# Row statistics over two rows at once, and the inverse root on VectorE instead of GpSimd, in the last layer of a graph network

## The reference, cut to what matters

```python
for l in range(4):                                  # 50000 nodes, 128 features, 25000 edges + self loops
    m = x @ weight[l]
    agg = segment_sum(m[src], dst, num_segments=50000)
    gi, gh = agg @ w_ih.T + b_ih, x @ w_hh.T + b_hh  # 3 x 128 each: r, z, n
    r, z = sigmoid(i_r + h_r), sigmoid(i_z + h_z)
    n = tanh(i_n + r * h_n)
    x = (1 - z) * n + z * x
y = x0 + (x + x0)                                   # x0: the input
out = (y - mean(y)) / sqrt(var(y) + 1e-5)           # over the 128 features
```

## Time and profile before

| | |
|---|---|
| median of three runs | 2330.25 us (2329.54 to 2333.68) |
| span of the profiled execution | 2327.4 us |
| what the median has beyond that span | 2.85 us |
| TensorE, VectorE busy | 96%, 93% of the span |
| ScalarE, GpSimd busy | 79%, 74% of the span |
| in 1900 to 2200 us, last layer: TensorE, VectorE | 294.04, 298.21 of 300 us |
| in the same stretch: ScalarE, GpSimd | 254.60, 258.29 of 300 us |

### The profile page before, as it was taken

One profiled execution on the slowest core, in us unless ns is written; L12 is line 12 of the kernel. 1 busy time (PEld: TensorE's weight loads), 2 busy tenths in 40 slices (PEclk: granted clock), 3 DMA queues, 4 the chain that ended last, 5 costly groups with the idle time before them and its releaser, 6 DMA issues.

```text
span 2327.4 us, 49180 instructions
## 1 busy us (share of the span) xinstructions
PE 2229.5 (96%) x11728; PEld 1898.3 (82%) x11728; DVE 2175.6 (93%) x4211; ACT 1842.3 (79%) x3483; POOL 1719.4 (74%) x1654
## 2 busy tenths in 40 slices
PE   3999999999999999999999999999989999999996
PEld 2888888888878888888878888888877888888885
DVE  7899999999879999999969999999969999999998
ACT  1688888888768888888857888888856888888886
POOL 3877777777487777777558777777748888888884
PEclk7999999999999999999999999999999999999998
DMA  2455555555545555555545555555544555555554
GB/s 58 120 155 160 158 160 161 158 160 160 157 131 173 171 173 172 174 172 173 166 127 172 172 171 172 173 174 171 174 130 122 159 156 155 155 155 154 155 155 118
DMA packets 277064, 362.45 MB, mean 156 GB/s; under 512 B 107754, under 2 KB 186586, under 8 KB 276980
## 3 DMA queue, kind: packets, MB, share of 16 engines
q1 hardware_dynamic: 238118, 309.12, 43.5%
q0 software_dynamic: 38784, 52.30, 9.7%
q10 hardware_dynamic: 78, 0.08, 0.0%
HBM read 208.71 MB, written 179.20 MB: 167 GB/s over the span
## 4 chain that ended last, share of the span: by engine, by line
PE 66%; DVE 18%; issue 10%; ACT 2%; DMA 2%; POOL 1%; DVEq 1%; SPq 0%; ACTq 0%; POOLq 0%
PE pZ L847 17%; PE pR L847 8%; PE pHN L847 8%; PE pA L835 8%; PE pO L929 5%; PE pIN L847 4%; PE pA L847 4%; DVE bn L1442 3%; PE pR L891 3%; PE pR L888 3%; PE pR L889 3%; DVE diff L1411 3%; DVE aggT L1381 3%; DVE y_rows L1435 2%; PE pH L786 2%
## 5 line engine op out<-in xcount | busy, mean ns | idle before, releaser
L683 POOL DMA_INDIRECT gath<-state,idx x900 | 931.4, 1035 | 264.6 <-issue 255.8
L660 POOL TENSOR_TENSOR h_lo<-hT,h_hi 128x500 fp32r<-128x500 f32 (+1 forms) x400 | 375.8, 940 | 200.5 <-ACT h_hi L1050 149.7
L683 POOL DMA_INDIRECT gath<-in_x_dram,idx x300 | 321.9, 1073 | 101.8 <-issue 68.7
L1080 ACT ACTIVATE rg<-pR,bsum 128x500 f32<-128x500 f32 x400 | 269.7, 674 | 112.2 <-PE pR L891 100.2
L1400 DVE SCALAR_TENSOR_TENSOR narg<-pHN,bhh,rg 128x500 f32<-128x500 f32 x400 | 292.3, 731 | 44.9 <-ACT rg L1080 44.1
L1372 DVE TENSOR_TENSOR a_lo<-aggT,a_hi 128x500 fp32r<-128x500 f32 x396 | 271.5, 686 | 0.3
L1062 ACT CAST sel<-sel 128x504 fp32r (+1 forms) x400 | 245.9, 615 | 31.6 <-DVE flag_i L1356 29.5
L1417 DVE TENSOR_TENSOR diff<-pZ,diff 128x500 f32<-128x500 f32 x400 | 267.7, 669 | 0.8
L1381 DVE TENSOR_TENSOR aggT<-pA,hT 128x500 f32<-128x500 f32 x396 | 263.8, 666 | 1.7 <-PE pA L835 1.6
L1088 ACT ACTIVATE pZ<-pZ,bsum 128x500 f32<-128x500 f32 x400 | 256.1, 640 | 0.0
L1067 ACT CAST a_hi<-aggT 128x500 fp32r<-128x500 f32 x396 | 235.6, 595 | 6.5 <-DVE aggT L1381 6.5
(11 more groups left out here) (211 smaller groups left out, 6384.1 us busy)
## 6 DMA issues: line engine op xcount, KB each, us to landing
columns<-newT SPq DMA_DIRECT2D x300, 250.0 KB, 2.3
hT<-columns SPq DMA_DIRECT2D x300, 250.0 KB, 2.7
state<-o_rows SPq DMA_DIRECT2D x300, 224.0 KB
x_rows<-in_x_dram SPq DMA_DIRECT2D x200, 224.0 KB
out_dram<-o_rows SPq DMA_DIRECT2D x91, 224.0 KB
gath<-state,idx POOLq DMA_INDIRECT x900, 2.4
state<-o_rows SPq DMA_DIRECT2D x297, 26.0 KB
idx<-edge_src SPq DMA_DIRECT2D x395, 1.5 KB
```

Of the source, the lines that this page charges most:

```text
L660: nc.gpsimd.tensor_tensor(part_of(h_lo, u)[:, cols], hT[:, u % RING, cols], part_of(h_hi, u)[:, cols].bitcast(F32), ALU.subtract).then_inc ...
L683: pool.indirect_dma_start(out=gath[:, u % RING, j, :], out_offset=None, in_=states[l], in_offset=bass.IndirectOffsetOnAxis(ap=idx[:, u % R ...
L1080: nc.scalar.activation(rg[:, :], pR[:, 0:COLS], ACT.Sigmoid, bias=bsum[:, 0:1]).then_inc(s_r, 1)
```

## The change

`row_stats` makes two `bn_stats` per block instead of four. Each reads two rows, one element of the one and one of the other in turn, so that the "even" part is the first row and the "odd" part the second: three values a row, mean and scaled variance at once. `moments` and `squared_difference` go, and `variance` is one operation. GpSimd makes no power. VectorE makes the inverse root in eight operations on 20 elements each: a guess from the integer bits, and two refinements. They stand one by one between the long operations of the step that follows the variance. `shift` stays where it was. The constants and `mhalf` change accordingly. The same is done for the two pieces at the end, where the eight stand in a row.

```diff
+MAGIC = float(0x5F1FFFF9 - (1 << 31))
+FIRST = 2.38924456
+SQUARED = 0.703952253 ** 2
+SCALED = 1.0 / (0.375 * 0.703952253) ** 2
+ROOTS = 8
...
-        bn = sb("bn", [ROWS, UNROLL, RPP, 6])
-        mv = sb("mv", [ROWS, UNROLL, RPP, 4])
+        bn = sb("bn", [ROWS, UNROLL, RPP, 3])
         veps = sb("veps", [ROWS, UNROLL, RPP])
         rstd = sb("rstd", [ROWS, UNROLL, RPP])
         nmr = sb("nmr", [ROWS, UNROLL, RPP])
-        mhalf = sb("mhalf", [ROWS, RING, RPP])
+        guess = sb("guess", [ROWS, RING, RPP])
+        near = sb("near", [ROWS, RING, RPP])
+        root_a = sb("root_a", [ROWS, RING, RPP])
+        root_b = sb("root_b", [ROWS, RING, RPP])
...
-            def root(s, k):
-
-                pool.wait_ge(s_eps, k + 1)
-                nc.gpsimd.tensor_tensor(rstd[:, s, :], veps[:, s, :], mhalf[:, 0:s.stop - s.start, :],
-                                        ALU.pow).then_inc(s_rstd, 1)
...
-                        half = half_done(i, u, RING + ROWLAG + 1) if l == L - 1 else None
-                        if half:
-                            root(*half)
...
-                for k in range(RPP):
-                    last = v.bn_stats(bn[:, u, k, :], y_rows[:, u, k * D:(k + 1) * D])
+                for r in range(0, RPP, 2):
+                    pair = y_rows[:, u, r * D:(r + 2) * D].rearrange("p (k d) -> p d k", k=2)
+                    last = v.bn_stats(bn[:, u, r:r + 2, :].rearrange("p k c -> p (k c)"), pair)
                 last.then_inc(s_bn, 1)
 
-            def moments(s, k, blocks_done):
+            def variance(s, blocks_done):
+
                 dve.wait_ge(s_bn, blocks_done)
-                v.tensor_tensor(mv[:, s, :, 0], bn[:, s, :, 1], bn[:, s, :, 4], ALU.add)
-                v.scalar_tensor_tensor(mv[:, s, :, 1], bn[:, s, :, 2], D * EPS, bn[:, s, :, 5], ALU.add, ALU.add)
-                v.tensor_tensor(mv[:, s, :, 2], bn[:, s, :, 1], bn[:, s, :, 4], ALU.subtract).then_inc(s_mv, 1)
-
-            def squared_difference(s, k):
-                dve.wait_ge(s_mv, 2 * k + 1)
-                v.scalar_tensor_tensor(mv[:, s, :, 3], mv[:, s, :, 2], 0.25, mv[:, s, :, 2],
-                                       ALU.mult, ALU.mult).then_inc(s_mv, 1)
-
-            def variance(s, k):
-
-                dve.wait_ge(s_mv, 2 * k + 2)
-                v.scalar_tensor_tensor(veps[:, s, :], mv[:, s, :, 1], 1.0 / D, mv[:, s, :, 3],
-                                       ALU.mult, ALU.add).then_inc(s_eps, 1)
+                v.tensor_scalar(veps[:, s, :], bn[:, s, :, 2], SCALED / D, SCALED * EPS, ALU.mult, ALU.add).then_inc(s_eps, 1)
+
+            def few(t, s):
+
+                return t[:, 0:s.stop - s.start, :]
+
+            def root_guess(s, k):
+                dve.wait_ge(s_eps, k + 1)
+                v.tensor_scalar(few(guess, s).bitcast(I32), veps[:, s, :].bitcast(I32), -0.5, MAGIC,
+                                ALU.mult, ALU.add).then_inc(s_root, 1)
+
+            def root_first(s, k, n):
+
+                dve.wait_ge(s_root, ROOTS * k + n)
+                if n == 1:
+                    ins = v.tensor_tensor(few(root_a, s), few(guess, s), veps[:, s, :], ALU.mult)
+                elif n == 2:
+                    ins = v.tensor_tensor(few(root_b, s), few(root_a, s), few(guess, s), ALU.mult)
+                else:
+                    ins = v.scalar_tensor_tensor(few(near, s), few(root_b, s), FIRST, few(guess, s), ALU.subtract, ALU.mult)
+                ins.then_inc(s_root, 1)
+
+            def root_second(s, k, n):
+
+                dve.wait_ge(s_root, ROOTS * k + n)
+                if n == 4:
+                    ins = v.scalar_tensor_tensor(few(root_a, s), few(near, s), SQUARED, veps[:, s, :], ALU.mult, ALU.mult)
+                elif n == 5:
+                    ins = v.tensor_tensor(few(root_b, s), few(root_a, s), few(near, s), ALU.mult)
+                elif n == 6:
+                    ins = v.scalar_tensor_tensor(few(root_a, s), few(root_b, s), 10.0 / 3.0, few(root_b, s),
+                                                 ALU.subtract, ALU.mult)
+                else:
+                    ins = v.scalar_tensor_tensor(rstd[:, s, :], few(root_a, s), 5.0, few(near, s), ALU.add, ALU.mult)
+                ins.then_inc(s_root, 1)
+
+            def root(s, k):
+                root_guess(s, k)
+                for n in range(1, 4):
+                    root_first(s, k, n)
+                for n in range(4, ROOTS):
+                    root_second(s, k, n)
 
             def shift(s, k):
 
-                dve.wait_ge(s_rstd, k + 1)
-                v.scalar_tensor_tensor(nmr[:, s, :], mv[:, s, :, 0], -0.5, rstd[:, s, :],
+                dve.wait_ge(s_root, ROOTS * (k + 1))
+                v.scalar_tensor_tensor(nmr[:, s, :], bn[:, s, :, 1], -1.0, rstd[:, s, :],
                                        ALU.mult, ALU.mult).then_inc(s_nmr, 1)
...
+                        rooted = half_done(i, u, RING + ROWLAG + 1) if final else None
                         shifted = half_done(i, u, OUTLAG) if final else None
                         ramp = isinstance(i, int) and i == 0 and u < RAMP
                         if last:
@@ -1509,24 +1531,34 @@
                         r_times_hn(l, b, u)
                         if shifted:
                             shift(*shifted)
+                        if rooted:
+                            root_guess(*rooted)
                         if not ramp and not last:
                             renew(*after(i, u, -1))
+                        if rooted:
+                            root_first(*rooted, 1)
                         n_argument(l, b, u)
+                        if rooted:
+                            root_first(*rooted, 2)
                         if ramp and u == 3:
                             low_part(l, 4, 4)
                         summed = after(i, u, 1 if ramp else 2)[:2] if exists(i, u, 2) else None
                         if summed and not (ramp and u == 3):
                             aggregate(l, *summed)
+                        if rooted:
+                            root_first(*rooted, 3)
                         if added and not ramp:
                             remainder(*after(i, u, -ROWLAG))
+                            if rooted:
+                                root_second(*rooted, 4)
                             row_stats(*after(i, u, -ROWLAG)[:2])
-                        if half:
-                            moments(*half, RING * (half[1] + 1))
+                        if rooted:
+                            root_second(*rooted, 5)
                         if l == 0 and exists(i, u, RAMP) and not ramp:
                             select(after(i, u, RAMP)[0])
                         difference(l, b, u)
-                        if half:
-                            squared_difference(*half)
+                        if rooted:
+                            root_second(*rooted, 6)
                         if not opening(i) and exists(i, u, 3) and not final:
                             low_gathered(l, *after(i, u, 3)[:2])
                         coming = on_from(l, i, u, PRE)
@@ -1535,13 +1567,15 @@
                             low_h(*coming[:3])
                         if summed and not (ramp and u == 3):
                             low_part(l, *summed)
+                        if rooted:
+                            root_second(*rooted, 7)
                         if ramp and u == 3:
                             aggregate(l, 5, 5)
                         product(l, b, u)
                         if coming and ramp:
                             low_h(*coming[:3])
                         if half:
-                            variance(*half)
+                            variance(half[0], RING * (half[1] + 1))
...
-                        moments(*ahead, NB - LATE)
-                        squared_difference(*ahead)
-                        variance(*ahead)
+                        variance(ahead[0], NB - LATE)
+                        root(*ahead)
                         for k in range(LATE, 0, -1):
                             remainder(NB - k, UNROLL - k, GROUPS - 1)
                             row_stats(NB - k, UNROLL - k)
                         shift(*ahead)
-                        moments(*late, NB)
-                        squared_difference(*late)
-                        variance(*late)
+                        variance(late[0], NB)
+                        root(*late)
```

More of the change, by code:

```diff
@@ L332, in build @@
         s_bn = sem("row_stats")
-        s_mv = sem("row_moments")
         s_eps = sem("variance_plus_eps")
-        s_rstd = sem("rstd_made")
+        s_root = sem("root_steps")
         s_nmr = sem("shift_made")
@@ L619, in _ @@
             nc.gpsimd.memset(gath[:, :, :, :], 0.0).then_inc(s_zero, 1)
-            nc.gpsimd.memset(mhalf[:, :, :], -0.5).then_inc(s_zero, 1)
             nc.gpsimd.memset(zeros[:, :], 0.0).then_inc(s_zero, 1)
@@ L625, in _ @@
```

(15 more changed lines are left out.)

## The result

The changed kernel takes 2344.66 us (median of 4 runs, 2343.48 to 2345.58); the kernel before, on the same chip, 2329.89 us (2328.87 to 2333.68, 4 runs). The ratio is 1.0058, 95% interval 1.0046 to 1.0069: slower by 14.8 us. The forecast was 2322.6 us, faster, with a range up to 2335. It was wrong in sign, and the time lies outside the range. The profiled spans are 2327.4 and 2341.8 us, 14.4 apart.

A forecast was written before the change was run, and what follows sets the result against it. VectorE sets the pace. Statistics 12.5 less 0.2 (ramp), 3.8 (small operations), 0.3 (last block but one) and 0.5 (end) make 7.7 us less: 2330.25 to 2322.6 us, range 2319.5 to 2335.

The forecast's parts named there:

- the one on GpSimd: Removing GpSimd's 19 powers of 3.57 us costs or saves nothing on the path, but keeps GpSimd from capping the gain.
- should have gaps that wait for VectorE: Sign expected in the profile after: GpSimd, with 25.3 us of work per five blocks, shows gaps waiting for VectorE.
- The small operations: Ten instead of six per half on VectorE, 0.095 us each: 0.84 against 0.64 us, 3.8 us more over 19 halves.
- The bounds given: One small VectorE operation takes at least 0.085 us and at most 0.21, the distance of two bare dependent ones.
- The statistics: Two paired `bn_stats` per block take 0.66 us instead of 0.79 on VectorE: 12.5 us less over 98 blocks.
- The fixed part: Part of a VectorE operation's time independent of length: 0.064 us, beside a slope of 1.04 ns per element.
- Rival 1: Reading two rows in turn is slower per element in the 98 pairs: 2379 us at 2.17 ns; chance 0.17.
- The end: Behind the last new state two root chains are each 1.1 us longer; the store queue hides most, 0.5 us more.
- Rival 2: Waits in the root's chain show, 0.21 us per small operation: 16 us slower, 2346 us; chance 0.06.
- Rivals 3 and 4: 3: another loop holds plain blocks at 5.65, 2334.5 us, chance 0.07; 4: GpSimd's power remains or is waited for, given nothing.

The follow-up runs named there:

- e1: The kernel before with GpSimd's power made a multiplication, VectorE's code untouched: 2342.72 us, ratio 1.0049.
- e2: The changed kernel with a spare power of 20 constants on GpSimd where the real one stood: 2346.18 us, ratio 1.0052 to the kernel before.
- e4: The changed kernel with its small operations moved so that none stands between `narg` and `newT` of a step: 2322.19 us, 0.9964 to the kernel before.
- e9: The changed kernel with `nmr` made at its place by a reduction reading `bn` alone: 2332.16 us, ratio 1.0005 to the kernel before.
- e5: The kernel before with the paired statistics and single variance operation alone, the power kept on GpSimd: 2334.99 us, ratio 1.0016.

## Why the prediction was wrong

**The step that failed is the one on GpSimd:** "19 powers of 3.57 us and two short ones go. Nobody waits for them, so their price on the path is nothing". It asked who waits for the power and not what GpSimd does with the time. The earlier trace rows had shown that GpSimd had no reserve, and the prediction read from it that the gain would not be capped. The power is also what had kept `h_lo` late, away from the place behind the product. e1 shows the price of the relief by itself: 11 us. The forecast even said that GpSimd "should have gaps that wait for VectorE", without asking what starts when such a wait ends.

**The small operations** carry that error in the sum: forecast 0.84 against 0.64 us per half, measured 1.98, which is 25 us instead of 3.8. Seven of the ten took 0.08 to 0.10, near the 0.095 forecast, and an eighth filled the wait in front of the statistics, as forecast. The held time of the other two is 19 x (0.41 + 0.69) = 20.9 us (572 and 868 ns, less the 165 and 177 that they take free). The bounds given, 0.085 to 0.21, were drawn from operations beside which no `h_lo` ran, so they left out what the two engines share.

**The statistics** were right in kind: a pair is read in 0.69 us instead of 0.79, 98 x 0.10 = 9.8 us, where 12.5 was forecast. The fixed part was set at 0.064 us; with 0.345 per operation and 256 elements at 1.04 ns it is 0.078. It could as well be the slope, 1.10 ns with 0.064 fixed, or 1.15 if it is drawn from the contiguous 128 elements at 0.1975: no run has a contiguous `bn_stats` of 256 elements, so what the 0.014 us are due to stays open. Rival 1, the slow jump, fell: it had asked for a record of 0.55 us or more, and the mean of 200 is 0.43. Of the prices per element that the prediction weighed, 1.04 is near, and 1.73 and 2.17 are not.

**The end** cost 0.3 of the 0.5 forecast, with steps of 0.20 us in the chains where 0.21 was forecast, and ScalarE waits once for `nmr`, 0.88 us, as forecast.

Together: -9.8 + 3.6 + 20.9 + 0.3 = +15.0 us (3.6 being 19 x 0.19, what is left of 1.98 - 0.64 without the held 0.44 + 0.71), against 14.4 between the spans. Single holds at the start of the last layer aren't in the sum (after, an `a_lo` of 1.88 us and the `near` of 1.38; before, an `a_lo` of 1.72), so it closes to some 2 us and no better. Rival 2 had named 2346 us, near the measured time, but by waits in the root's chain at 0.21 each; these were 0.09. Being near in number doesn't make it right. Rivals 3 and 4 fell too: the plain block went to 5.55, and no power was left.

What stays open: why e2's `root_a`, whose record starts first, is held, and why the power and the gathers don't hold what `h_lo` does. A form of `guess` that doesn't use both ports wasn't tried.

## What to carry to other kernels

Relieving an engine is a change of its own: ask what it will start earlier and what stands there on its neighbour. Between VectorE and GpSimd look at inputs: a small VectorE operation with two SBUF inputs, or a `tensor_scalar`, placed where GpSimd starts a long elementwise operation on SBUF costs that operation's rest, here 0.5 to 1.3 us instead of 0.09. Put such operations elsewhere (e4: 22.5 us less than the changed kernel, for the same instructions), or use a kind that doesn't hold (e9).

## What the runs showed of the hardware

- The hold is seen only in lengths: no idle time and no wait is charged. A record that is longer than that of the same operation with nothing beside it (868 against 161 ns for `nmr`) is the sign, and the start of the next operation says what it cost: in e2 `veps` has a record of 0.34 us beside a gather (2017.21), but the next operation starts 0.08 us after it.
- It holds GpSimd too. In e2 the gather of 2016.10 began beside VectorE's `a_lo` of 2016.03 and took 1.47 us, the next one 1.00; in e5 one of 2014.63 took 1.27. In the last layer of the kernel before, 18 gathers began 0.25 to 0.32 us after an `a_lo` and took 1.23 to 1.32 us; another 18, begun 0.5 us after one or later, took their usual 0.99 to 1.03.
- The power (3.57 us on 20 elements) doesn't hold VectorE: `a_lo` takes 0.67 us beside it.
- A `bn_stats` with one SBUF input isn't held: in e5 the pair of 2001.98 ran its usual 0.77 us within an `h_lo` of 2001.91 to 2002.99.
- `bn_stats` reading two rows in turn costs 0.345 us for 256 elements: 0.014 more than the 0.331 worked out from contiguous reads, so 1.04 to 1.15 ns per element, by what is taken as its fixed part.
- Dependent small operations with nothing between are 0.20 us apart, with one long operation between them 0.09.
